# Two-layer conditioned transformer: set-up reordered, and in even attention steps the row maxima transposed ahead of the step's scores

## The reference

```python
mod = silu(c) @ w_adaln + b_adaln                   # (16, 6*144)
sh_msa, sc_msa, g_msa, sh_mlp, sc_mlp, g_mlp = split(mod, 6, axis=-1)
h = modulate(ln(x), sh_msa, sc_msa)
q, k, v = (h @ w_qkv + b_qkv)                       # 16 heads of 9
attn = softmax(q @ k.T * 9 ** -0.5)
x = x + g_msa[:, None, :] * ((attn @ v) @ w_proj + b_proj)
xn = modulate(ln(x), sh_mlp, sc_mlp)
moe = sum over the top 2 of 4 experts of gate * (gelu(xn @ w1 + b1) @ w2 + b2)
x = x + g_mlp[:, None, :] * moe                     # layer 1: a plain gelu MLP in its place
```

## Time and profile before

| | |
|---|---|
| median of 3 runs | 477.94 us (473.98, 477.94, 478.56) |
| the profiled execution | 475.46 us, of which the span from first to last instruction is 473.6 us |
| mean granted TensorE clock | 0.964 of full |
| PE busy | 419.0 us (88%) |
| DVE busy | 279.1 us (59%) |
| ACT busy | 273.4 us (58%) |
| POOL busy | 131.8 us (28%) |

### The profile page before, as it was taken

The page is one execution under the profiler, slowest core; times in us unless marked ns, Lnnn a source line. Parts: engine busy times, 40 slices in busy tenths (PEclk is TensorE's granted clock), DMA queues, the critical chain, the costliest instruction groups (busy, mean ns, idle before and its releaser), DMA issues.

```text
span 473.6 us, 10747 instructions
## 1 busy us (share of the span) xinstructions
PE 419.0 (88%) x4010; PEld 339.6 (72%) x4010; DVE 279.1 (59%) x796; ACT 273.4 (58%) x515; POOL 131.8 (28%) x217
## 2 busy tenths in 40 slices
PE   3775489898889999999998999998899998889997
PEld 1443368677667779878976897798677786768885
DVE  7864467588964326359622763267676566764652
ACT  4433178887586690383067336813678865867562
POOL 3203144253211063036008300714152432121000
PEclk9987589999999999999999999999799998999999
DMA  7944344546544000100000215203336475210112
GB/s 208 213 130 147 103 143 140 152 122 180 159 128 128 21 1 2 26 0 1 0 27 1 51 27 162 88 2 77 120 92 186 142 173 148 72 39 3 51 50 76
DMA packets 51566, 42.51 MB, mean 90 GB/s; under 512 B 33587, under 2 KB 43754, under 8 KB 51510
## 3 DMA queue, kind: packets, MB, share of 16 engines
q1 hardware_dynamic: 51450, 41.80, 31.7%
q0 software_dynamic: 64, 0.02, 0.0%
HBM read 33.20 MB, written 8.29 MB: 88 GB/s over the span
## 4 chain that ended last, share of the span: by engine, by line
PE 54%; DVE 12%; ACT 11%; issue 9%; DMA 6%; SPq 6%; POOL 3%; DVEq 0%; ACTq 0%; POOLq 0%
PE bank L1688 14%; PE bank L1706 4%; PE s_pair L1527 3%; PE bank L1569 2%; PE st_pair L1550 2%; DMA QA<-mT 2%; PE s_pair L1466 2%; PE s_pair L1467 2%; PE s_pair L1473 2%; PE s_pair L1470 2%; PE st_pair L1466 2%; DVE mx L1259 2%; PE st_pair L1467 2%; PE st_pair L1473 2%; PE bank L1579 2%
## 5 line engine op out<-in xcount | busy, mean ns | idle before, releaser
L1259 DVE TENSOR_REDUCE mx<-s_pair 128x8 f32<-128x1024 f32 x62 | 75.7, 1221 | 37.4 <-PE s_pair L1527 36.8
L1688 PE MATMUL bank<-w_sb,hid 128*128 128x144 f32 x640 | 80.5, 286 | 0.9 <-DVE aT L1338 0.9
L1688 PEld LDWEIGHTS bank<-w_sb,hid 128*128 128x128 f32 x640 | 79.6, 190 | 1.8 <-DVE aT L1338 1.2
L965 ACT ACTIVATE pr<-st_pair 128x1024 f32<-128x1024 f32 x64 | 65.9, 1029 | 24.4 <-PE st_pair L1550 24.1
L1014 ACT ACTIVATE hid<-s_pair 128x512 f32<-128x512 f32 x40 | 23.3, 612 | 51.4 <-PE s_pair L1473 51.4
L1527 PE MATMUL s_pair<-KA,QA 81*128 81x128 bf16 x400 | 34.0, 233 | 9.6 <-issue 5.5
L1569 PE MATMUL bank<-pr,V 128*10 128x128 f32 x1024 | 41.1, 280 | 0.0
L1527 PEld LDWEIGHTS s_pair<-KA,QA 81*128 81x128 bf16 x400 | 26.7, 104 | 16.9 <-issue 12.5
L1550 PE MATMUL st_pair<-QA,KA 83*128 83x128 bf16 x416 | 34.0, 228 | 4.1 <-DMA QA<-mT 4.1
L792 POOL TENSOR_TENSOR rstd<-var_eps,minus_half 128x4 f32<-128x4 f32 x16 | 16.3, 1018 | 75.6 <-DVE var_eps L1213 75.5
L836 POOL TENSOR_TENSOR xs<-xs,tmp 128x144 f32<-128x144 f32 x32 | 17.1, 533 | 64.3 <-DVE tmp L1280 38.8
(11 more groups left out here) (279 smaller groups left out, 961.0 us busy)
## 6 DMA issues: line engine op xcount, KB each, us to landing
QA<-qk_scratch SPq DMA_DIRECT2D x25, 324.0 KB
KA<-qk_scratch SPq DMA_DIRECT2D x75, 108.0 KB
qk_scratch<-parts SPq DMA_DIRECT2D x16, 288.0 KB, 3.8
g_att<-gate_scratch SPq DMA_DIRECT2D x16, 144.0 KB, 4.1
g_mlp<-gate_scratch SPq DMA_DIRECT2D x8, 288.0 KB, 4.0
hid<-qk_scratch SPq DMA_DIRECT2D x6, 324.0 KB
hid<-qk_scratch SPq DMA_DIRECT2D x18, 108.0 KB
qk_scratch<-parts SPq DMA_DIRECT2D x16, 96.0 KB, 3.4
```

The source lines that it names most:

```text
L965: sc.activation(pr[:, Pn % 2, :], st_pair[:, :], ACT.Exp, scale=SCALE).then_inc(s["exp_s"], 1)
L1259: v.tensor_reduce(mx[:, HP * h:HP * (h + 1)], src[:, :].rearrange("p (h k) -> p h k", k=SEQ), AX.X, ALU.max).then_inc(s["max_s"], 1)
L1688: last = te.matmul(dst, hid[:, at:at + SEQ], w2_sb[:, MT1 * e + i, :], start=(i == 0), stop=(i == MT1 - 1))
```

## The change

1. In even steps `MAX_T` is yielded ahead of `MAX`, for all steps and not only for `p <= 0`. PE thus transposes the last batch's maxima before it computes the step's scores.
2. `H_REST` of a coming group (at `r == -14`) and `H_MAIN` of the first group of the second half (at `r == 4`) go into a new list `post`, behind `PV`. The split of that group comes one step later (`r == 7`).
3. Set-up: the product of modulation half (0, 1) and its copy move ahead of the first `QK` product. All three `QK` products and first casts of group 0 come ahead of the second casts. Piece (0, 1)'s `part_c` goes from POOL to DVE. `GATES 0` comes ahead of the two `STORE_R` and of the loads, and the value weights of layer 0 later. Modulation half (1, 1) is computed into `SMALL` (bank 7) ahead of `QK (1, 0)`, and the wait of the first scores for `gate_c` 4 goes over to the first `MAX_T`.
4. The first store of `mT` in each layer is issued by ACT and no longer by POOL.

```diff
-        MODT_BANK = ((bank[1], bank[4]), (bank[2], bank[0]))
+        MODT_BANK = ((bank[1], bank[4]), (bank[2], SMALL))
...
                     if r == -14:
-                        late.append(("H_REST", n))
+                        post.append(("H_REST", n))
...
-                    if i == NG and r in (4, 5, 6):
-                        late.append((("H_MAIN", "H_REST", "H_SPLIT")[r - 4], n))
+                    if i == NG and r == 4:
+                        post.append(("H_MAIN", n))
+                    if i == NG and r in (5, 7):
+                        late.append(("H_REST" if r == 5 else "H_SPLIT", n))
...
-            if p <= 0 and h == 0 and 0 <= b + 1:
+            if h == 0 and 0 <= b + 1 < BATCH:
                 yield "MAX_T", B0 + b + 1
             if p + LEAD < NP:
                 yield "MAX", P0 + p + LEAD
-            if p > 0 and h == 0 and b + 1 < BATCH:
-                yield "MAX_T", B0 + b + 1
...
             if 0 <= p - 1:
                 yield "PV", P0 + p - 1
+            yield from post
...
-            yield "QK", (0, 0)
             yield "STATS", 1
-            yield "PART_R", (0, 0)
+            for t in range(PARTS):
+                yield "QK", (0, t)
+                yield "PART_R", (0, t)
             yield "PART_B", (0, 0)
             yield "STORE", (0, 0)
             yield "MOMENTS", 1
-            yield "QK", (0, 1)
-            yield "PART_R", (0, 1)
             yield "PART_B", (0, 1)
+            yield "PART_C", (0, 1)
             yield "STORE", (0, 1)
-            yield "WEIGHTS_V", 0
-            yield "QK", (0, 2)
-            yield "PART_R", (0, 2)
             yield "PART_B", (0, 2)
-            yield "APPLY", (1, (0, 1))
             yield "PART_C", (0, 2)
             yield "STORE", (0, 2)
+            yield "GATES", 0
             yield "STORE_R", (0, 1)
             yield "STORE_R", (0, 2)
+            yield "WEIGHTS_V", 0
+            yield "APPLY", (1, (0, 1))
             yield "APPLY", (1, (2, 3))
-            yield "MOD", (0, 1)
+            yield "MODT", (0, 1)
             yield "V", (0, 0)
             yield "V", (0, 1)
-            yield "MODT", (0, 1)
             yield "H_MAIN", 1
+            yield "H_REST", 1
+            yield "MOD", (1, 0)
             yield "SPLIT_M", 1
-            yield "H_REST", 1
             yield "SPLIT_R", 1
+            yield "MOD", (1, 1)
...
-            yield "GATES", 0
-            yield "MOD", (1, 0)
...
-            yield "MOD", (1, 1)
...
-            def store_max(B):
-
-                pool.wait_ge(s["mt_c"], B + 1)
-                gp.dma_start(QAs[slot_of(B)][SROWS:MROWS, :, :], mT[:, :]).then_inc(s["m_first"], 16)
...
-                if what == "PART_B" and i != (0, 2):
+                if what == "PART_B" and i not in ((0, 1), (0, 2)):
                     part_c(*i)
...
+            def store_first_max(B):
+
+                act.wait_ge(s["mt_c"], B + 1)
+                sc.dma_start(QAs[slot_of(B)][SROWS:MROWS, :, :], mT[:, :]).then_inc(s["m_first"], 16)
...
             h_round(0)
             rest_round(0)
+            mod_out(0, 1)
...
                 if Pn == 0:
-                    pe.wait_ge(s["gate_c"], 4)
                     pe.wait_ge(s["h_rest"], 2)
...
                 if B % BATCH == 0:
-                    need(pe, *(("v_ready", 2) if B == 0 else ("gate_s", 4 * NG)))
+                    need(pe, *(("gate_c", 4) if B == 0 else ("gate_s", 4 * NG)))
...
                 if L == 1:
-                    need(pe, *(("part_r", 3) if half == 0 else ("mod_read", 2)))
+                    need(pe, *(("part_r", 3) if half == 0 else ("v_ready", 2)))
...
                 transposes(0, True)
+                modulation(0, 1)
```

More of the change, by code:

```diff
@@ L220, in prep_order @@
             a0 = NG * L
-            pre, first, mid, late = [], [], [], []
+            pre, first, mid, late, post = [], [], [], [], []
             for i in range(1, G + 2):
@@ L302, in prep_order @@
                 late.append(("UP_PE", (L, 0, (p - NP + 3) // 2)))
-            return pre, first, mid, late
+            return pre, first, mid, late, post
         def attention_step(L, p):
@@ L308, in attention_step @@
             b, h = p // PAIRS, p % PAIRS
-            pre, first, mid, late = prep_order(L, p)
+            pre, first, mid, late, post = prep_order(L, p)
             yield from pre
@@ L878, in _ @@
                     max_split(i // PAIRS)
-                if what == "MAX_T" and i % BATCH == 0:
-                    store_max(i)
                 if what == "PROJ":
@@ L1062, in _ @@
                     m_out(i)
+                    if i % BATCH == 0:
+                        store_first_max(i)
                 if what == "SCORE":
```

## The result

The changed kernel has a median of 471.36 us (469.73 to 472.70, 4 executions) against 476.19 us of the kernel before on the same chip: ratio 0.9897, 95% interval 0.9849 to 0.9945. It is faster by 2.5 to 4.8 us, where 11 to 12 were forecast.

What follows compares the result with a forecast made beforehand. PE, the busiest engine, was taken to lose time from 30 to 55 us to a chain of waits and a lowered clock. Terms 8.4 + 3.0 = 11.4 us off 475.46 gave 464.1; it said 466, range 460 to 474.

Steps and rivals of the forecast that it cites:

- the 6.3 us at the first maximum: Set-up: first maximum starts at 37.9 instead of 44.27 us, 2.3 of it from scores no longer waiting for the bank.
- the 8.4 us of the set-up: Set-up through first transposed scores: 6.3 at the first maximum, 1.6 for ACT's store, 0.5 for the full clock.
- DVE's last low part follows five us after this cast, as before: Group 1 in the set-up: last low part at 37.9 us, five us after ACT's first cast at 32.9.
- The first cast at 32.9: Group 1's first cast on ACT in the set-up: starts at 32.9 instead of 36.95 us, 4.0 us earlier.
- The 0.5 us for the full clock at the first maxima: Between the first maxima: three scores each 0.4 us shorter at full clock, 1.2 in all, of which 0.5 counted.
- Rival 1: PE keeps its clock through first maxima and steps 0 to 2: 2.8 us more gain, 463 us; chance 0.15.
- The 4.0 us of the gates: Set-up: with the gates stored ahead of the loads, group 1's first cast starts at 32.9 instead of 36.95 us.
- The later split and `post`: Attention steps 24 to 27: less waiting by PE, 1.5 us per layer, 3.0 us in all, between 0 and 4.
- ACT's store: First store of the maxima: lands before the fourth maximum ends, so transposed scores follow at once, 1.6 us gained.
- Rival 3: Steps 2 to 6 wait for loads; the 8.4 us becomes 4 or vanishes: 474 to 477 us; chance 0.10.
- the second (part is given back): Groups 2 and 3 delayed, group 0 at low clock, nothing from steps 24 to 27: 4.3 us gain, 473.5; chance 0.18.
- The slower case: Each of 28 even attention steps waits 0.57 us for POOL's split: 16 us lost, 482 us; chance 0.07.

Runs made afterwards that it cites:

- run 2: Kernel before with only the gates' store moved ahead of the two other stores and the eight loads: 475.67 us, ratio 0.9968.
- the first two experiments: Changed kernel with group 1's pieces ahead of group 2's layer norm on DVE: 469.35 us, ratio 0.9821; and run 2.
- run 11: Changed kernel with five extra products, read by nothing, where PE waits for the value weights: 471.52 us, ratio 0.9885.
- run 8: Changed kernel once more, unedited, for a second trace and more timed executions: 473.72 us, ratio 0.9928.
- run 3: Kernel before with only the last modulation half moved to bank 7 and its wait moved to the first `MAX_T`: 474.39 us, ratio 0.9941.
- run 4: Kernel before with only each layer's first store of the maxima issued by ACT instead of POOL: 477.19 us, ratio 0.9997.
- run 10: Changed kernel with group 1's pieces ahead of group 2's layer norm, plus layer 0's value weights back ahead of the second store: 471.99 us, ratio 0.9909.

## Why the prediction was wrong

The direction was right and the size was not: 466 us was forecast, 471.4 and 473.7 were measured, an effect of 2.5 to 4.8 us instead of 11.4.

**The term that failed is the 6.3 us at the first maximum**, inside the 8.4 us of the set-up. The first transposed scores moved from 54.99 to 52.31 in the mean of five traces, 2.7 us. What is missing, 5.7 us, has three parts:
- *"DVE's last low part follows five us after this cast, as before"* was false. It ends 7.8 us after the cast (34.28 to 42.12), since group 2's layer norm stands ahead of the first subtraction. Before, this work ran while ACT waited for the gates and ended 0.84 us before the subtraction (run 2), so the same list of items cost nothing. I had asked what PE and ACT would meet once the gates were early, and not what DVE had in its queue. This is 2.8 us. The Trainium skill (PSUM — Partial Sum Buffer, Engine vs sequencer instructions) says that the queues of ScalarE, VectorE and GpSimdE are strictly first in, first out; by that rule the 2.8 us could have been read from the order of the changed program, and the first two experiments agree with it (3.46 us between cast and subtraction against 0.61).
- *The first cast at 32.9* came at 35.3 in the mean, 2.4 us late. I moved the value weights behind all of group 0 in my account ("the transposes of group 1 start 0.9 later") and did not ask what PE would do meanwhile: it idles for 4.5 us and runs the V products and transposes at the half clock, 1.3 us (run 11). The rest, about 1.1, I put down to the rise of the clock in group 0's products; no edit tested it, but the first casts of the five traces come in the order of their rises. The rise was forecast for 18 or 19 us; it came at 16 in one trace of the five and at 19.5 to 20.8 in four.
- *The 0.5 us for the full clock at the first maxima* did not come: the clock was 0.50 from 40 to 48 us, and from the first maximum to the end of the fourth it took 9.01 us (9.03 before). Rival 1, the clock that recovers, failed with it.

So the part of the set-up that paid is the bank and its wait, as forecast: 2.3 us were put down to it, and alone it brought 2.85 at the first maximum. The 4.0 us of the gates were worth 0.9 at the subtraction (run 2). All set-up changes together brought 1.2 at the first maximum (44.27 to 43.05), less than the bank alone, so the rest of them cost more than it gave in the changed kernel as it stands. The first subtraction shows it too: 38.74 us in the mean of the five traces against 37.56 before, although the gates alone brought it to 36.64. How these 2 us divide among the other moves and the late rise of the clock was not tested one by one. The comparison with the bank alone rests on a single trace of the bank alone, and its ratio (0.9941) does not settle it.

**What was right.** The maxima ahead were taken as 0, between +1.7 and -2: at equal clock they gave 0.1 ± 0.8. In steps 2 and 10 `post` was put at 0; the wait for `osb` that it removed there was 1.02 us at step 10, and a wait for a load took its place (run 8). The later split and `post` were 3.0 us for both layers and measured 2.7 (2 x 1.37) in the traces, 1.8 ± 0.7 at equal clock, and the place, DVE's split just ahead of a maximum, was the right one. ACT's store was to end the wait behind the fourth maximum (1.6 us): it did so in four traces of five, though with a quick transfer POOL's issue left only 0.27 us of it too (50.02 to 50.29, run 3). My landing time for it, 3.06 or 4.03 us by SP's rows, was too short: 4.41 and 5.35 were measured. (POOL's 4.98 is the time to the landing at 54.86; the scores began 0.13 later.) By the prediction's estimate from the Trainium skill (DMA: Bandwidth & Descriptors, Latency and other measured facts), 0.4 us less than POOL's, it would be 4.58. The runs neither bear this out nor refute it: POOL's three transfers took 3.54, 4.98 and 5.46 us, so that the spread within one engine is wider than the difference. What ACT's issue surely gives is the 0.7 to 0.8 us by which it comes sooner. The spread of the three runs before, given as 4.8 us in the prediction, is 4.6 (473.98 to 478.56); nothing hangs on it.

**What the time adds up to.** 2.7 at the first transposed scores and 2.7 in the steps are 5.4 us. The executions say 4.7 at equal clock (both sets together), and the changed kernel's mean clock, 0.958 against 0.961, takes back 0.7 of that. Between 5.4 and 4.7 there may be what run 4 showed, a gain ahead of layer 0's steps that is gone by the 25th maximum. In the kernel before, the stretch from the first transposed scores to the 25th maximum took 65.8 us, in the 13 others 66.5 to 69.4. Two things in the traces bear on this. The half clock lasts on behind the first transposed scores, 7.7 us in the kernel before and 8.7 in the first trace of the changed one, and up to the 15th maximum it takes 33.3 us in the trace with the least of it (7.4, run 3) and 34.0 in those with the most (9.4, runs 2 and 11): starting sooner under the half clock gives back up to half a microsecond. And behind the 15th maximum stands the wait for the load that run 8 shows. Rival 3, the loads, did not occur in steps 2 to 6, where no trace has PE waiting for one. With one trace of the kernel before, I can't tell how much of the rest is that this trace was a quick one; that stays open.

Of the rivals, the second (part is given back) named the right size, 473.5, in part by the wrong causes: it had the later steps worth nothing, delays of groups 2 and 3, and the low clock in group 0's products. The first was wrong (2.7 us in the traces), the second was seen at one load (0.2 to 2.1 us, against 0.28 before), and the last came half true, at 1.1 us of its 1.7. The slower case did not occur: PE waited for POOL's split twice, both times at the start of a layer.

## What to carry to other kernels

When a wait is removed, read the queue of the next engine in the new order before putting down the gain: work that was free inside the old wait now stands in the path. How long that next engine had been idle when the old wait ended, here 0.84 us, is about what removing the wait can give. A reordering that left PE idle for 4.5 us cost twice here, in the gap and in the clock behind it; a few useless products there were worth 1.3 us at the first cast, though the medians (471.52 against 473.72 us) lie within the noise of each other. And where the clock moves single executions by 6 us, compare several traces of the same stage, or the time at equal clock, before believing a landmark.

## What the hardware showed that I had not expected

- With the same set-up, PE's clock rose from 1.2 to 2.4 GHz in group 0's products by 16 us or at 19.5 to 20.8 us (the unedited kernel had 16 and 19.6), and with it the first maximum moved by up to 1.6 us. The Trainium skill (TensorE: Matmul & The Clock Gate, What's actually happening) says that the number of slow matmuls at a kernel's start varies from run to run; the traces agree, with a wider spread than the half a microsecond either way that it gives for the transition.
- The second set of the changed kernel has executions of 469.05 us (clock 0.967) and of 475.34 us (0.950). A good part of the spread of a one-core kernel went with the clock (correlation -0.74 over 88 executions of the kernel before). A half-clock stretch in the middle of dense steps (92 to 96 us, above) was there in one trace, behind a wait of 2.08 us for a load, and not in the other trace of the same kernel, where PE waited 0.90 us.
- A shorter idle stretch did not give back the clock: 2.31 us of waiting and, later, 1.40 (run 10) were followed by a longer half-clock stretch, 23 to 39 us, than 4.50 us of waiting (22 to 29 us), with PE busy without a gap from 29 us on.
- The first store of the maxima in layer 0, 8 KB, took 4.41, 4.87 and 5.35 us in three traces when ACT issued it, and 3.54, 4.98 and 5.46 in three when POOL did.
